# Values and softmax sums of two heads in one product, in the three attentions of a decoder kernel

## The chip, the cores and the metric

The kernel runs on one core of a Trainium2 chip. A core has a matmul engine (TensorE, PE in the profile, its weight loads PEld), VectorE (DVE), ScalarE (ACT), GpSimd (POOL), and SyncE (SP), which here only issues DMAs. The metric is the device time of one execution in microseconds (us); lower is better.

## What is computed

A decoder of two layers on 16 sequences of 256 tokens with 256 features, in float32: a differential causal self attention (32 heads of 16 features), a cross attention (16 heads), a mixture of experts, a state space block, a causal attention against the context (16 heads), and a feed-forward with low-rank experts, each with a residual and a layer norm. The change touches the three attentions. For each head they compute

```python
scores = q @ k.T / 4                   # 256 x 256, masked above the diagonal in self and causal
p = exp(scores - row_max(scores))
o = (p @ v) / p.sum(-1, keepdims=True) # 16 features a head
y = o_all_heads @ w_out
```

## The kernel before

Each attention is a software pipeline over the 16 batches. One pass of the loop body goes through `PAIRS` pairs of heads (16 in self, 8 in cross and causal, one "pair" `i` being one step of the body), and works on several batches at once: `st.has(d)` asks whether batch `st + d` exists, so `d = 3` is a batch whose projections are made, `d = 1` one whose row maxima are taken, `d = 0` one whose scores and products run, `d = -1` and `-2` batches on their way out. The order of work on each engine is written out by hand, as `if i == ...` in five `body` functions, one for each engine. Engines meet through counting semaphores.

For each pair:

- TensorE computes the scores of the pair into the single PSUM tile `score_ps` (`scores`, L522 in cross and causal, L1180 in self); it waits for `prob_ready` of the pair before.
- ScalarE takes the exponential into one of four `probs` buffers (`exponential`, L632, L1278). In self and causal GpSimd then zeroes the masked half of the diagonal blocks (`mask_probs`, L1494, L815).
- TensorE computes the score products of the next batch into one of two `max_ps` banks (`max_scores`), and VectorE takes the row maxima from them (`take_max`, L1415/L1416, L722). Four pairs' maxima are transposed (`transpose_max`), copied by ScalarE (`keep_max`) and sent into the row `TERMS` of the stacks by a small DMA from ScalarE's queue (`load_row`, L622, L1259), 4 KB and 8 KB. The first scores of each four pairs (i = 0, 4, ...) wait for that row.
- At every second pair TensorE runs `weighted` for a group `g` of two pairs: four heads in four 32-wide column tiles (`quad`). The parity `par` of the group says which half of the 32 rows of a quad holds the head. A tile of `out_ps` (128 rows, 512 columns) holds eight heads' values in its columns 0 to 255 and their softmax sums, from products with `ones`, in 256 to 511. Two groups (par 0 and 1) accumulate into it.

When both groups of a tile are there, ScalarE copies `out_ps` to `comb` (`keep_weighted`, L639, L1286), after the exponential of pair 2 or 6 (self also 10 and 14). VectorE inverts the sums and multiplies (`normalize`, L731 and L735, L1423 and L1427). GpSimd splits the result in a high and a low part (`part_o`, a cast and a subtraction, L824 and L826, L1503 and L1505), and TensorE projects it (`output` at i = 2 in cross and causal, `output_1` at i = 14 in self, by `product3`, L79 to L81). There are two tiles a batch in cross and causal and four in self. VectorE's `norm_rows` adds the residual and takes the moments, GpSimd takes `rstd` (`pow`), VectorE `shift_rows`, and ScalarE's `finish_rows` writes `y_out` (L648 at i = 6, L1310 at i = 7).

GpSimd in self also sorts a quarter of the queries twice a batch (`sort_q`, L1534, i = 1 and 9) and the keys (`sort_k`, L1525, i = 15), splits the queries (`split_q`, L1541, i = 6 and 8) and the low part of the keys (L1564, i = 11), and pads the values (`pad_v`, i = 10). ScalarE sorts the other quarters (L1269, i = 5 and 14) and rounds (L1301).

SyncE's order in cross and causal, for each pass: the residual rows, the next tokens and context, the first half of the stacks (which waits for `q_saved`), the store of `y_out` (which waits for `out_ready`), the save of k, the second half of the stacks, the save of q. Its queue is in order: what stands behind a wait waits too.

## Time and profile before

| | |
|---|---|
| time, median of 3 runs | 2770.53 us (2765.45 to 2774.43) |
| span of the profiled execution | 2765.9 us |
| TensorE busy | 2451.4 us (89%), weight loads 2025.2 us (73%) |
| VectorE busy | 1928.7 us (70%) |
| ScalarE busy | 1439.0 us (52%) |
| GpSimd busy | 1560.7 us (56%) |
| DMA | 363.48 MB, mean 131 GB/s |

The profile is of one execution; its time is its span, and no other time is given for it. Self attention fills its first 722 us, cross attention runs to about 1108 us, causal attention from about 2140 to 2510 us. Busy shares are means over stages whose limits differ, and an engine's idle time costs something only where the next engine waits for it. The granted clock (PEclk) is a share of TensorE's full 2.4 GHz; its two levels are 1.00 and 0.50.

### The profile page before, as it was taken

The page shows a single profiled execution, that of the slowest core. Times are in us where ns is not written, and L with a number is a line of the kernel's source. Part 1 is how long each engine was busy: PE and PEld are TensorE (multiplying, and loading weights), DVE is VectorE, ACT ScalarE, POOL GpSimd, SP SyncE. Part 2 cuts the span into 40 slices and gives each one's busy share as a digit, 9 for nine tenths or more (in the row PEclk, how much of TensorE's full clock was granted, in tenths as well). Part 3 has the DMA queues.
Part 4 walks back from the last instruction along what each step waited for, and adds up shares of the span by engine and source line. Part 5 has one row for each costly group of instructions (what it writes and reads, how often), then busy time and mean ns, then how long its engine had stood idle before and what let it go on. Part 6 is the DMA issues. An engine that isn't in the chain of part 4 may idle for free. (4 is left out here: it accounts for less than half of the span.)

```text
span 2765.9 us, 66315 instructions
## 1 busy us (share of the span) xinstructions
PE 2451.4 (89%) x24760; PEld 2025.2 (73%) x24760; DVE 1928.7 (70%) x3095; ACT 1439.0 (52%) x2255; POOL 1560.7 (56%) x1873
## 2 busy tenths in 40 slices
PE   5999999999589998898999994888896799997998
PEld 4676666676466665898999993677775577765998
DVE  2567666677367786364888885999985377775776
ACT  2565565565356665433665663656563355553333
POOL 3666565666345543056666664777765477764443
PEclk9999999999799999899999997999997899998999
DMA  8565555562477873024666663111000877761111
GB/s 200 124 152 138 130 146 117 144 146 68 122 193 203 208 193 93 31 89 160 217 230 221 216 217 118 37 39 47 24 13 29 238 192 207 209 146 35 58 57 50
DMA packets 228039, 363.48 MB, mean 131 GB/s; under 512 B 52848, under 2 KB 157168, under 8 KB 220272
## 3 DMA queue, kind: packets, MB, share of 16 engines
q1 hardware_dynamic: 207248, 281.28, 38.9%
q0 software_dynamic: 17376, 78.13, 8.0%
q8 instruction: 153, 2.51, 0.4%
q10 hardware_dynamic: 3200, 1.05, 0.2%
q14 instruction: 62, 0.51, 0.1%
HBM read 231.68 MB, written 133.69 MB: 132 GB/s over the span
## 5 line engine op out<-in xcount | busy, mean ns | idle before, releaser
L1278 ACT ACTIVATE self_probs<-self_score_ps 128x768 f32<-128x768 f32 x256 | 207.7, 811 | 218.7 <-PE self_score_ps L1180 215.7
L1494 POOL TENSOR_SCALAR_AFFINE_SELECT self_probs<-self_probs 128x512 f32<-128x512 f32 x256 | 167.7, 656 | 217.6 <-ACT self_probs L1278 217.4
L1415 DVE TENSOR_REDUCE self_neg_max<-self_max_ps 128x2 f32<-128x256 f32 x256 | 108.2, 422 | 227.1 <-PE self_max_ps L1166 223.6
L722 DVE TENSOR_REDUCE cross_neg_max<-cross_max_ps 128x4 f32<-128x1024 f32 x128 | 155.9, 1222 | 70.6 <-PE cross_max_ps L500 69.6
L632 ACT ACTIVATE cross_probs<-cross_score_ps 128x1024 f32<-128x1024 f32 x128 | 131.1, 1024 | 92.9 <-PE cross_score_ps L522 92.8
L1416 DVE TENSOR_REDUCE self_neg_max<-self_max_ps 128x2 f32<-128x512 f32 x256 | 174.5, 682 | 0.0
L2206 POOL TENSOR_TENSOR moee_h_lo<-moee_h,moee_h_hi 128x512 fp32r<-128x512 f32 x78 | 112.0, 1436 | 93.0 <-ACT moee_h_hi L1943 92.3
L3501 POOL TENSOR_TENSOR ffn_g_lo<-ffn_g_full,ffn_g_hi 128x512 fp32r<-128x512 f32 x64 | 82.2, 1284 | 129.4 <-ACT ffn_g_hi L3387 117.0
L1943 ACT ACTIVATE moee_h_hi<-moee_h 128x512 fp32r<-128x512 f32 x110 | 69.5, 632 | 164.2 <-DVE moee_h L2109 158.7
L632 ACT ACTIVATE causal_probs<-causal_score_ps 128x768 f32<-128x768 f32 x128 | 103.9, 811 | 95.0 <-PE causal_score_ps L522 94.9
L1180 PE MATMUL self_score_ps<-self_q_stack,self_k_stack 49*128 49x128 f32 (+1 forms) x1024 | 131.3, 336 | 24.7 <-issue 10.3
L79 PE MATMUL moee_g_ps<-moee_x_hi,moee_in_hi 128*128 128x256 f32 x440 | 132.2, 300 | 11.1 <-DVE moee_x_lo L2096 6.9
L1180 PEld LDWEIGHTS self_score_ps<-self_q_stack,self_k_stack 49*128 49x128 f32 x1024 | 79.0, 191 | 73.6 <-issue 40.0
L2109 DVE TENSOR_TENSOR moee_h<-moee_u_ps,moee_silu 128x512 f32<-128x512 f32 x110 | 75.6, 687 | 81.2 <-PE moee_u_ps L81 77.0
L1160 PE MATMUL self_max_ps<-self_k_stack,self_q_stack 48*128 48x128 f32 (+1 forms) x1024 | 108.2, 291 | 23.0 <-POOL self_k_stack L1525 22.0
L815 POOL TENSOR_SCALAR_AFFINE_SELECT causal_probs<-causal_probs 128x512 f32<-128x512 f32 x128 | 85.0, 664 | 75.7 <-ACT causal_probs L632 71.8
L79 PE MATMUL moee_y_ps<-moee_out_hi,moee_h_hi 128*128 128x256 f32 x440 | 125.3, 285 | 1.5 <-DVE moee_out_lo L2061 1.5
L81 PE MATMUL moee_g_ps<-moee_x_hi,moee_in_lo 128*128 128x256 f32 x440 | 126.4, 287 | 0.0
L80 PE MATMUL moee_g_ps<-moee_x_lo,moee_in_hi 128*128 128x256 f32 x440 | 126.3, 287 | 0.0
L2149 POOL DMA_INDIRECT x_tiles<-kept_x,moek_slot x64 | 65.8, 1029 | 106.7 <-issue 103.0
L79 PE MATMUL moee_u_ps<-moee_x_hi,moee_in_hi 128*128 128x256 f32 x440 | 125.5, 285 | 0.0
L81 PE MATMUL moee_u_ps<-moee_x_hi,moee_in_lo 128*128 128x256 f32 x440 | 125.0, 284 | 0.0
(500 smaller groups left out, 9667.4 us busy)
## 6 DMA issues: line engine op xcount, KB each, us to landing
self_q<-self_q_split SPq DMA_DIRECT2D x48, 512.0 KB, 3.2
self_q_raw<-self_q SPq DMA_DIRECT2D x32, 768.0 KB, 7.9
cross_stacks<-cross_qk SPq DMA_DIRECT2D x64, 384.0 KB, 6.6
causal_stacks<-causal_qk SPq DMA_DIRECT2D x64, 384.0 KB, 6.6
moe_y_tiles<-lasting_y_out SPq DMA_DIRECT2D x55, 256.0 KB, 2.5
mid<-lasting_y_out SPq DMA_DIRECT2D x48, 256.0 KB, 2.2
x_tiles<-zeros SPq DMA_DIRECT2D x16, 624.0 KB, 4.5
moee_xT<-x_tiles SPq DMA_DIRECT2D x39, 256.0 KB, 7.1
```

The source lines that it names most:

```text
L79: pe.matmul(out, a[0], b[0], start=start, stop=False, **kw)
L80: pe.matmul(out, a[0], b[1], start=False, stop=False, **kw)
L81: return pe.matmul(out, a[1], b[0], start=False, stop=stop, **kw)
L632: nc.scalar.activation(probs[i // 2][:, a, :, lo:], score_ps[:, :, lo:], ACT.Exp, scale=HD ** -0.5).then_inc(prob_ready, 1)
L722: last = dve.tensor_reduce(neg_max[p][:, tile, :, col % 4, :], bank[:].rearrange("p a (q k) -> p a q k", q=QT), AX.X, ALU.max, negate=True)
L1160: last = pe.matmul(max_ps[i % 2][:, ab, q * S:q * S + (q + 1) * P], q_stack[rows, 4 * tile + c, q * P:(q + 1) * P], k_stack[p][rows, tile, ...
L1180: last = pe.matmul(score_ps[:, ab, j * S + k * P:(j + 1) * S], k_stack[p][rows, tile, k * P:(k + 1) * P], q_stack[rows, 4 * tile + c, k * P:],
L1278: nc.scalar.activation(probs[g % 4][:, a, :, P:], score_ps[:, :, P:], ACT.Exp, scale=HD ** -0.5).then_inc(prob_ready, 1)
L1415: dve.tensor_reduce(neg_max[:, tile, :, c, 0:1], bank[:, :, 0:P], AX.X, ALU.max, negate=True)
L1416: dve.tensor_reduce(neg_max[:, tile, :, c, 1:2], bank[:, :, S:2 * S], AX.X, ALU.max, negate=True).then_inc(max_kept, 1)
L1494: pool.affine_select(diagonal, diagonal, [[0, 2], [0, 2], [1, P]], ALU.is_ge, zero, base=0, channel_multiplier=-1).then_inc(prob_masked, 1)
L2206: pool.tensor_tensor(h_lo[p][f][:].rearrange("p j s -> p (j s)"), h[f][:], h_hi[p][f][:].bitcast(F32).rearrange("p j s -> p (j s)"), ALU.s ...
```

## The change

A `weighted` group now has one set of eight matmuls instead of two. The unused half of each 32-column tile of `v_pad`, zero before, holds ones in every second of its 16 columns (the even ones for an even tile, the odd ones for an odd tile), so that the product gives the head's 16 values and, in eight of the other 16 rows, its softmax sum. The two groups of a tile no longer accumulate: par 0 goes to columns 0 to 255 of `out_ps`, par 1 to 256 to 511, and values and sums of the two lie in opposite halves of each 32 rows.

To bring them together, ScalarE (`cross_weighted`) copies `out_ps` with its two column halves exchanged and one row half zeroed by a column `scale`, into `crossed`. VectorE (`merge`) multiplies `out_ps` by the other column and adds `crossed`, into `merged`: values in one column half, sums in the other. A tile's sums sit in every second row, with zeros between them. GpSimd adds the sums of two tiles (`add_sums`, into `merged[0]`), VectorE inverts both at once (`invert`), and `normalize` spreads a tile's inverses over the rows, exchanging the row halves, with `stream_shuffle`, behind a one-column memset, and multiplies. `comb_ready`, which frees `out_ps` for TensorE, becomes `merged_ready`.

Places: `cross_weighted` stands ahead of the exponential of its pair, not behind it. `merge` is at the same pairs (2 and 6; 2, 6, 10, 14 in self); cross and causal: `add_sums` at 2, `invert` at 4, `normalize` at 5 and 6, `part_o` at 6 and 7 (before: normalize at 4 and 7, part_o at 3 and 5). Self: `add_sums` at 2 and 10, `invert` at 4 and 11, `normalize` at 5, 6, and both at 11 (before 3, 7, 11, 15), `part_o` at 6, 7, 12, 13 (before 0, 4, 8, 12). `pad_v` in self copies instead of adding zeros. The diff, cut to its core (cross and causal first, then self):

```diff
-        self.ones = m.sb("ones", [P, 2, 32])
+        self.halves = m.sb("halves", [P, 2])
...
-        comb = [m.sb(f"comb{i}", [P, 2, S]) for i in range(2)]
-        inv_sum = m.sb("inv_sum", [P, 2, S])
+        crossed = [m.sb(f"crossed{i}", [P, 2, S]) for i in range(2)]
+        merged = [m.sb(f"merged{i}", [P, 2, S]) for i in range(2)]
+        sums, inv_sum = merged[0][:, 1, :], merged[1][:, 1, :]
...
-                    pe.wait_ge(comb_ready, st.at(d) * 2 + tile)
-                for part in range(4):
-                    k = part % 2
-
+                    pe.wait_ge(merged_ready, st.at(d) * 2 + tile)
+                for k in range(QT):
                     first_q = P if causal and k == 1 else 0
                     cols = slice((1 - k) * S + first_q, (2 - k) * S)
                     for quad in range(4):
                         rows = slice(32 * quad, 32 * quad + 32)
-                        if part < 2:
-                            lhs = v_pad[p][:, k, tile * 4 + quad, par, :, :].rearrange("p a e -> p (a e)")
-                            out0 = 0
-                        else:
-                            lhs, out0 = ones[:, par, :], S
-                        last = pe.matmul(out_ps[rows, out0 + first_q:out0 + S], lhs,
+                        lhs = v_pad[p][:, k, tile * 4 + quad, par, :, :].rearrange("p a e -> p (a e)")
+                        last = pe.matmul(out_ps[rows, par * S + first_q:(par + 1) * S], lhs,
                                          probs[g][:, quad % 2, quad // 2, cols],
-                                         start=(par == 0 and part == 0),
-                                         stop=(par == 1 and part == 3), skip_group_check=True)
+                                         start=k == 0, stop=k == QT - 1, skip_group_check=True)
                 last.then_inc(pv_done, 1)
...
-            def keep_weighted(st, d, tile):
+            def cross_weighted(st, d, tile):
                 act.wait_ge(pv_done, st.at(d) * 4 + 2 * tile + 2)
                 if st.has(d - 1):
                     act.wait_ge(o_ready, st.at(d) * 2 + tile - 1)
-                nc.scalar.activation(comb[tile][:].rearrange("p a s -> p (a s)"), out_ps[:],
-                                     ACT.Identity).then_inc(comb_ready, 1)
+                nc.scalar.activation(crossed[tile][:, ::-1, :], out_ps[:].rearrange("p (a s) -> p a s", s=S),
+                                     ACT.Identity, scale=halves[:, 1:2]).then_inc(crossed_ready, 1)
...
+                    if i == 2 and st.has(-1):
+                        cross_weighted(st, -1, 1)
+                    if i == 6 and st.has(0):
+                        cross_weighted(st, 0, 0)
                     if st.has(0):
                         exponential(st, i)
...
-                    if i == 2 and st.has(-1):
-                        keep_weighted(st, -1, 1)
-                    if i == 6 and st.has(0):
-                        keep_weighted(st, 0, 0)
                     if i == 6 and st.has(-2):
                         finish_rows(st)
...
+            for t in range(2):
+                for tile in range(2):
+                    for par in range(2):
+                        ones = v_pad[t][:, :, 4 * tile:4 * tile + 4, par, 1 - par, tile::2]
+                        last = dve.memset(ones, 1.0)
+                last.then_inc(v_zeroed, 1)
...
+            def merge(st, d, tile):
+
+                dve.wait_ge(crossed_ready, st.at(d) * 2 + tile + 1)
+                if st.has(d - 1):
+                    dve.wait_ge(sums_ready, st.at(d))
+                    dve.wait_ge(o_ready, st.at(d) * 2 + tile - 1)
+                dve.scalar_tensor_tensor(merged[tile][:], out_ps[:].rearrange("p (a s) -> p a s", s=S),
+                                         halves[:, 0:1], crossed[tile][:], ALU.mult, ALU.add).then_inc(merged_ready, 1)
+
+            def invert(st, d):
+                dve.wait_ge(sums_ready, st.done(d))
+                dve.reciprocal(inv_sum, sums).then_inc(inv_ready, 1)
+
             def normalize(st, d, tile):
 
                 n = st.at(d) * 2 + tile
-                dve.wait_ge(comb_ready, n + 1)
-                dve.reciprocal(inv_sum[:, tile, :], comb[tile][:, 1, :]).then_inc(inv_ready, 1)
-                dve.wait_ge(inv_ready, n + 1)
+                dve.wait_ge(inv_ready, st.done(d))
+                dve.memset(gate[:], 0.0)
+                dve.stream_shuffle(crossed[tile][:, 1, :], inv_sum, [HD + tile] * HD + [tile] * HD).then_inc(scale_ready, 1)
+                dve.wait_ge(scale_ready, n + 1)
                 if st.has(d - 1):
                     dve.wait_ge(olo_ready, n - 1)
-                dve.tensor_tensor(o_full[:, tile, :], comb[tile][:, 0, :], inv_sum[:, tile, :],
+                dve.tensor_tensor(o_full[:, tile, :], merged[tile][:, 0, :], crossed[tile][:, 1, :],
                                   ALU.mult).then_inc(o_ready, 1)
...
+                    if i == 2 and st.has(-1):
+                        merge(st, -1, 1)
+                    if i == 6 and st.has(0):
+                        merge(st, 0, 0)
                     if i == 3 and st.has(-2):
                         norm_rows(st)
+                    if i == 4 and st.has(-1):
+                        invert(st, -1)
+                    if i in (5, 6) and st.has(-1):
+                        normalize(st, -1, i - 5)
                     if i == 5 and st.has(3):
                         dve.wait_ge(xhi_ready, st.done(3))
                         dve.tensor_tensor(x_lo[:].rearrange("p k s -> p (k s)"), misc[:],
@@ -772,10 +795,6 @@
                                           ALU.subtract).then_inc(xlo_ready, 1)
                     if i == 5 and st.has(-2):
                         shift_rows(st)
-                    if i == 4 and st.has(-1):
-                        normalize(st, -1, 1)
-                    if i == 7 and st.has(0):
-                        normalize(st, 0, 0)
...
+            def add_sums(st, d):
+                pool.wait_ge(merged_ready, st.done(d) * 2)
+                if st.has(d - 1):
+                    pool.wait_ge(inv_ready, st.done(d - 1))
+                pool.tensor_tensor(sums, merged[0][:, 1, :], merged[1][:, 1, :], ALU.add).then_inc(sums_ready, 1)
...
+                    if i == 2 and st.has(-1):
+                        add_sums(st, -1)
...
-                    if i == 3 and st.has(-1):
-                        part_o(st, -1, 0)
-                    if i == 5 and st.has(-1):
-                        part_o(st, -1, 1)
+                    if i in (6, 7) and st.has(-1):
+                        part_o(st, -1, i - 6)
...
+                    if i in (2, 6, 10) and st.has(0):
+                        cross_weighted(st, 0, i // 4 + 1)
+                    if i == 14 and st.has(1):
+                        cross_weighted(st, 1, 0)
...
-                    if i in (2, 6, 10) and st.has(0):
-                        keep_weighted(st, 0, i // 4 + 1)
-                    if i == 14 and st.has(1):
-                        keep_weighted(st, 1, 0)
...
-                    if i in (3, 7, 11) and st.has(0):
-                        normalize(st, 0, i // 4 + 1)
+                    if i in (2, 6, 10) and st.has(0):
+                        merge(st, 0, i // 4 + 1)
+                    if i in (4, 11) and st.has(0):
+                        invert(st, 0, i // 8)
+                    if i in (5, 6) and st.has(0):
+                        normalize(st, 0, i - 5)
+                    if i == 11 and st.has(0):
+                        normalize(st, 0, 2)
+                        normalize(st, 0, 3)
+                    if i == 14 and st.has(1):
+                        merge(st, 1, 0)
...
-                    if i == 15 and st.has(1):
-                        normalize(st, 1, 0)
...
+            def add_sums(st, d, half):
+                n = st.at(d) * 2 + half
+                pool.wait_ge(merged_ready, 2 * n + 2)
+                if half or st.has(d - 1):
+                    pool.wait_ge(inv_ready, n)
+                pool.tensor_tensor(sums, merged[0][:, 1, :], merged[1][:, 1, :], ALU.add).then_inc(sums_ready, 1)
...
-                    zeros = v_pad[p][:, :, par, 1 - par, :]
-                    pool.tensor_tensor(v_pad[p][:, :, par, par, :], v_nat[:], zeros,
-                                       ALU.add).then_inc(v_padded, 1)
+                    pool.tensor_copy(v_pad[p][:, :, par, par, :], v_nat[:]).then_inc(v_padded, 1)
...
-                    if i in (0, 4, 8, 12) and st.has(0):
-                        part_o(st, 0, i // 4)
+                    if i in (2, 10) and st.has(0):
+                        add_sums(st, 0, i // 8)
+                    if i in (6, 7, 12, 13) and st.has(0):
+                        part_o(st, 0, (6, 7, 12, 13).index(i))
...
-    a["ones"] = np.broadcast_to(np.repeat(np.eye(2), HD, axis=1), (P, 2, 2 * HD)).astype(np.float32)
+    a["halves"] = np.stack([i % 32 < HD, i % 32 >= HD], 1).astype(np.float32)
```

## Rows read from the trace of the kernel before

**Rows 1.** Busy time by stage; columns: PE, PEld, DVE, ACT, POOL, clock, DMA.
```profile
77.00:722.00 645.00, 601.65 (x7793) 436.78 (x7792) 432.61 (x767) 371.25 (x558) 389.18 (x509) 0.96 0.52 124
...
779.00:1108.00 329.00, 304.45 (x3764) 215.85 (x3762) 248.27 (x319) 201.82 (x296) 148.62 (x217) 0.99 0.69 174
```

**Rows 2.** TensorE in order of time in self: start, length, line, instructions.
```profile
387.25 0.83 PE L1205 MATMUL self_out_ps<-self_probs,lasting_ones 128*32 128x256 f32 x16
388.01 0.50 PE L1180 MATMUL self_score_ps<-self_q_stack,self_k_stack 49*128 49x128 f32 x4
...
395.37 0.50 PE L1180 MATMUL self_score_ps<-self_q_stack,self_k_stack 49*128 49x128 f32 x4
...
411.42 0.37 PE L79 MATMUL self_misc<-self_wo_hi,self_o_hi 128*128 128x256 f32 x1
```

**Rows 3.** ScalarE in order of time in self, pairs 5 and 6.
```profile
391.91 2.06 ACT L1269 ACTIVATE self_q_stack<-self_q_raw 128x1024 fp32r<-128x1024 f32 x1
...
394.38 0.81 ACT L1278 ACTIVATE self_probs<-self_score_ps 128x768 f32<-128x768 f32 x1
```

**Rows 4.** TensorE in self at the first max product of a batch; bracket: idle, releaser.
```profile
418.72 0.50 PE L1160 MATMUL self_max_ps<-self_k_stack,self_q_stack 48*128 48x128 f32 x4 [1.33 <-POOL self_k_stack L1525]
```

**Rows 5.** Busy time in two stretches of cross; last columns: clock, DMA share, GB/s.
```profile
938.00:950.00 12.00, 11.13 (x135) 8.29 (x136) 8.83 (x14) 6.02 (x10) 5.73 (x10) 1.00 1.04 265
953.00:956.00 3.00, 3.00 (x36) 2.60 (x36) 1.94 (x3) 2.49 (x5) 2.64 (x4) 1.00 0.00 0
```

**Rows 6.** SyncE's longest wait in cross: total us, times, longest.
```profile
SPq L396 <- ACT lasting_y_out L648: 132.5, 15, 15.9
```

**Rows 7.** TensorE in order of time in cross.
```profile
940.66 1.05 PE L547 MATMUL cross_out_ps<-cross_probs,lasting_ones 128*32 128x256 f32 x16
941.63 0.51 PE L522 MATMUL cross_score_ps<-cross_stacks 49*128 49x256 f32 x4
...
947.39 0.50 PE L522 MATMUL cross_score_ps<-cross_stacks 49*128 49x256 f32 x4 [0.87 <-DMA cross_stacks<-cross_max_row]
```

**Rows 8.** Instructions of ScalarE's copy in self; ns min/median/max, first and last start.
```profile
L1286 ACT ACTIVATE self_comb<-self_out_ps x64: 575/592/620, 86.2 to 711.1; 128x512 f32<-128x512 f32 x64
```

**Rows 9.** ScalarE's groups in self: busy us, mean ns, idle before.
```profile
L1310 ACT ACTIVATE lasting_y_out<-self_r,self_shift,self_rstd 128x256 f32<-128x256 f32 x30 | 16.5, 610 | 0.0
```

**Rows 10.** VectorE in order of time in self, pairs 3 to 5.
```profile
387.62 0.68 DVE L1437 TENSOR_TENSOR self_r<-self_misc,self_x_res 128x512 f32<-128x512 f32 x1
...
389.52 1.75 DVE L1423 RECIPROCAL self_inv_sum<-self_comb 128x256 f32<-128x256 f32 x1
391.31 0.42 DVE L1427 TENSOR_TENSOR self_o_full<-self_comb,self_inv_sum 128x256 f32<-128x256 f32 x1
391.65 0.42 DVE L1415 TENSOR_REDUCE self_neg_max<-self_max_ps 128x2 f32<-128x256 f32 x1
...
392.58 0.42 DVE L1415 TENSOR_REDUCE self_neg_max<-self_max_ps 128x2 f32<-128x256 f32 x1
```

**Rows 11.** GpSimd's groups in self: busy us, mean ns, idle before.
```profile
L1494 POOL TENSOR_SCALAR_AFFINE_SELECT self_probs<-self_probs 128x512 f32<-128x512 f32 x253 | 165.8, 656 | 210.4 <-ACT self_probs L1278 210.2
L1534 POOL CAST self_q_stack<-self_q_raw 128x1024 fp32r<-128x1024 f32 x30 | 60.1, 2002 | 0.0
L1505 POOL TENSOR_TENSOR self_o_lo<-self_o_full,self_o_hi 128x256 fp32r<-128x256 f32 x64 | 46.8, 731 | 5.4
L1541 POOL TENSOR_TENSOR self_q_split<-self_q_full,self_q_split 128x512 fp32r<-128x512 f32 x26 | 33.3, 1279 | 0.0
...
L1503 POOL CAST self_o_hi<-self_o_full 128x256 fp32r<-128x256 f32 x64 | 25.2, 394 | 34.4 <-DVE self_o_full L1427 34.4
...
L1564 POOL TENSOR_TENSOR self_k_split<-self_k_full,self_k_split 128x256 fp32r<-128x256 f32 x14 | 10.2, 728 | 0.0
```

**Rows 12.** Busy time and clock in self behind the wait of rows 4.
```profile
420.00:424.00 4.00, 4.00 (x39) 2.38 (x42) 2.22 (x5) 1.41 (x2) 2.94 (x4) 0.50 0.43 96
```

**Rows 13.** TensorE at the end of cross, its last output product.
```profile
1103.47 0.55 PE L79 MATMUL cross_misc<-cross_w_hi,cross_o_hi 128*128 128x256 f32 x1 [5.66 <-POOL cross_o_lo L826]
```

More of the change, by code:

```diff
@@ L1191, in weighted @@
                 if par == 0 and (tile or st.has(d - 1)):
-                    pe.wait_ge(comb_ready, st.at(d) * TILES + tile)
-                for part in range(4):
-                    k = part % 2
+                    pe.wait_ge(merged_ready, st.at(d) * TILES + tile)
+                for k in range(QT):
                     first_q = P if k == 1 else 0
```

66 lines of the change are left out of this document (42 added, 24 removed).

## The prediction

> **What bounds the kernel now.** I read the stages first, then each engine in order of time inside one batch, then waits. In the stage table [rows 1] TensorE is busy for 602 of 645 us in self attention and 304 of 329 us in cross attention; causal attention reads like cross. One would say: TensorE bound, take its work away and time falls with it. The views in order of time say otherwise. TensorE's order is written by hand and each pair's scores go through one PSUM tile, so scores i+1 wait for ScalarE's exponential i. What fills TensorE between two scores is cover for the other engines, and three things behind that cover are nearly as long as it is:
>
> - ScalarE in self, pairs 5 and 6: the q_stack copy (2.06 us) and a rounding stand ahead of exponential 6, which ends at 394.38 + 0.81 = 395.19; TensorE's next scores start at 395.37 [rows 2, 3]. Slack 0.2 us.
> - GpSimd in self: TensorE stands 1.33 us before the max products of the next batch, until sort_k is done [rows 4]. That chain (exponential 15, mask, sort_k) hangs on scores 15, not on the product behind them.
> - The DMA engines in cross (and causal): 1.04 share, 265 GB/s, for 12 us, then 0.00 for 3 us [rows 5]. The burst starts when the y_out store, which SyncE waits for (132.5 us in 15 waits), is released by finish_rows at pair 6 [rows 6]. The small row of maxima that scores 4 need lands when the burst has drained: TensorE waits 0.87 us for it [rows 7].
>
> **The products.** Per group of pairs eight matmuls with `ones` (16 records in the trace) go. In self they take 388.01 - 387.25 = 0.76 us, in cross 941.63 - 940.66 = 0.97 us [rows 2, 7]. Groups: 8 x 16 = 128 in self, 4 x 16 = 64 in cross and 64 in causal (priced as self: it too skips the masked half). Ceiling: 128 x 0.76 + 64 x 0.97 + 64 x 0.76 = 97 + 62 + 49 = 208 us. Part of each 0.76 is the turn to the next scores, which stays; I walk with 0.7 and 0.9.
>
> **The added work.** ScalarE's copy becomes one of the same size with a scale column and swapped halves: 0.59 us [rows 8]; no row has a scaled 128x512 copy, so between 0.59 and twice the 0.61 us of finish_rows' scaled 128x256 (1.22) [rows 9]; I take 0.6, since only a column is added. It also moves ahead of the exponential of its pair. merge on VectorE (128x512, PSUM and SBUF) is nearest to self_r, 0.68 us [rows 10]. add_sums on GpSimd is like o_lo, 0.73 us [rows 11]. The reciprocal (1.75 us) runs half as often: 4 to 2 per batch in self, 2 to 1 in cross and causal. The shuffle (128x256) has no row: 0.42 us as the multiply of the same size, which reads one tensor more, up to the reciprocal's 1.75 [rows 10]; below 0.42 I see nothing, as every 256-column row of VectorE is at least that. I take 0.42, since a shuffle does no arithmetic. VectorE per self batch: -2 x 1.75 + 4 x 0.68 + 4 x 0.42 = +0.9 us; cross and causal: -1.75 + 2 x 0.68 + 2 x 0.42 = +0.45. In self, pad_v's two adds (as k_low, 0.73) become copies (as o_hi's cast, 0.39 [rows 11]): 0.7 us off GpSimd. The eight setup memsets lie beside the weights' loading, and the new memset of one column rides in front of each shuffle.
>
> On the shuffle, the Trainium skill ("VectorE: DVE Perf Modes", The perf-mode tier table) says that it exists only in the one-element-per-cycle mode. Its formula for fp32 tensor_tensor gives an estimated 0.42 us at 256 columns; the multiply's row agrees, and no run here shows a shuffle yet.
>
> **Self, walked from scores 4 (time 0).** Now scores 7 start at 395.37 - 388.01 = 7.36 [rows 2]. With product 3 shorter, norm_rows ends on VectorE 0.6 later relative to scores 4 than now (reciprocal start, 389.52 - 388.01 = 1.51 [rows 10]), at 2.1. Then take_max 4 (392.58 - 391.65 = 0.93 [rows 10]) to 3.0, invert to 4.8, take_max 5 to 5.7, shift_rows to 6.1, shuffle and multiply of tile 0 to 7.1. The new copy of pair 6 waits for exactly that (o_ready), and exponential 6 stands behind it: 7.1 + 0.6 + 0.8 gives scores 7 at 8.6. So the product at pair 5 saves nothing, and 1.3 us are lost.
> From there GpSimd decides. Until output_1 (pair 14) it has 8 masks x 0.66, 4 part_o x (0.39 + 0.73) instead of 2, 2 split_q x 1.28, sort_q 2.0, k_low 0.73, pad_v 0.8 and add_sums 0.73 [rows 11]: 5.3 + 4.5 + 2.6 + 2.0 + 0.7 + 0.8 + 0.7 = 16.6 us. TensorE needs now 411.42 - 395.37 = 16.05 [rows 2], after four shorter products 16.05 - 2.8 = 13.3. So TensorE stands about 3 us in front of output_1, partly already before max_scores 14, because invert and two normalizes hold VectorE at pair 11 for 1.75 + 2 x 0.9 = 3.6 us in front of take_max 12. That makes output_1 1.3 + 0.7 = 2.0 us later than now. Product 15 is hidden by sort_k. Products 1 and 3 of the next batch save 1.4 together, more where the clock is low. Net per batch: 0, from -0.5 to +1. Five of eight shortened products are eaten where they stand, the others pay back what the chain lost.
>
> **Cross and causal.** Products 1 and 3 lie between scores 0 and scores 4, which wait for the drained burst: both save nothing and the wait grows from 0.87 to about 2.5 us. The burst starts with finish_rows, behind exponential 6, behind the new copy, behind o_ready of tile 0: from scores 4, take_max 4 ends at 2.0, invert 3.8, take_max 5 4.9, normalize 5.9, copy 6.5, exponential 7.5. Against now this is 0.2 us (cross) to 0.4 us (causal, whose take_max is shorter) earlier, though products 5 and 7 save 1.8. The loop burst, scores 4, finish_rows closes with a gain of 0.2 to 0.4 per batch.
>
> **The clock.** After a 1.33 us idle stretch the granted clock is 0.50, 1.2 instead of 2.4 GHz, for the next 4 us [rows 4, 12]. A mean clock of 0.96 over self's 645 us [rows 1] is 52 us at half rate, 3 us in each of 16 batches, while the 0.87 us of rows 7 leaves 1.00. The change makes idle stretches of 2 to 3 us in front of output_1 and in front of scores 4 of cross and causal, where TensorE is then on the path. Four us at half rate cost up to 2 us each. Charged at half, with less where chains of other engines cover it: self +1.0, cross +0.5, causal +0.4 per batch net of the gains above.
> The Trainium skill ("TensorE: Matmul & The Clock Gate", HAM oscillation) says that waits between groups of matmuls let the gate fall, so that each next group starts at half rate. That is the rule that speaks against removing matmuls without removing the wait; the 0.50 row agrees.
>
> **Stage ends.** After the last product the chain to the output grows by merge 0.7, add_sums 0.7, shuffle and multiply of a second tile 0.9 and a second part_o 1.1, less what ran beside: TensorE's 5.66 us wait [rows 13] becomes about 8. Three stages: +6.
>
> **Sum.** With 14 full batches in self and 13 each in cross and causal: 14 x 1.0 + 13 x 0.5 + 13 x 0.4 + 6 = 14 + 6.5 + 5 + 6 = +31 us. The profiled execution's span is 2765.9 us, 4.6 under the median of the three runs (2770.5), as near as the runs stand to each other. 2765.9 + 31 = 2797, against the median 2802; I say 2800. A measurement of this kernel can tell about 0.3%, 8 us, from no change.
>
> **Rivals.** (a) The chains hold as walked but no further stretch loses its clock: self 0, cross -13 x 0.2, causal -13 x 0.4, ends +6: 2768 (2755 to 2778). Against it: the 1.33 us stretch already costs the clock. (b) Faster: tile 0 is normalized before TensorE reaches pair 6, so the copy never waits and finish_rows moves with TensorE. It decides if VectorE finishes 1.1 us earlier. Then products 5 and 7 pay in cross and causal (26 x 1.5 = 40 us) and in self about 2 of the 8 products (14 x 1.5 = 21), less some clock: 2705, from 2660 to 2745. For it: VectorE idles elsewhere in each batch. Against: the order in its queue is fixed. The floor is the DMA work, about 17 of 21 us in cross. (c) Worse: scaled copy 1.2 us or shuffle 1.75 us: each tile adds 0.6 or 1.3 to the chain before exponential 6 or output_1; 40 batches x 1 to 1.5 us on top of the forecast: 2850. (d) TensorE is the bound after all: 128 x 0.7 + 64 x 0.9 + 64 x 0.7 = 192 us less, 2580.
>
> **Chances.** Forecast 0.43 (2780 to 2830, slower); (a) 0.24 (same 0.15, faster 0.06, slower 0.03); (b) 0.23; (c) 0.06; (d) 0.04. Sum: faster 0.33, same 0.15, slower 0.52. The range 2715 to 2835 leaves out (c), (d) and a part of (b), about 2 in 10.
>
> **What the profile after would show.** 4,096 matmul records fewer and TensorE busy some 190 us less; VectorE about 16 x 0.9 + 32 x 0.45 = 29 us more; exponential 6 in self and finish_rows behind o_ready of tile 0; in cross a wait of 2 us or more at scores 4 for the row of maxima with a clock of 0.50 behind it; in self a wait at max_scores 14 or output_1. I am wrong if the y_out store in cross comes over 1 us earlier in its batch, if output_1 starts without a wait, or if idle stretches of 2 us keep the clock at 1.00.

## The result and the profile after

The changed kernel needs 2857.9 us (median of 4 runs, 2850.6 to 2863.6), the kernel before, on the same chip, 2770.6. The ratio is 1.031 (95% interval 1.028 to 1.033): 87 us slower, where 31 were forecast and the range ended at 2835. The profiled execution took 2852.6 us with a span of 2850.7 and a mean granted clock of 0.891 (before 0.943).

The page of the changed kernel, busy times and the line of the granted clock:

```profile
PE 2405.1 (84%) x20664; PEld 1985.6 (70%) x20664; DVE 1956.0 (69%) x3567; ACT 1453.6 (51%) x2255; POOL 1590.2 (56%) x1937
...
PEclk8788888888779998799999997999998799987999
```

The 4,096 matmul records are gone, yet TensorE is busy for only 46 us less, not 190: what is left runs slower. The windows by stage give the place (columns as in [rows 1]). First self attention from its first to its last exponential, then the same for cross, then causal:

```profile
65.00:762.00 697.00, 601.41 (x5749) 432.38 (x5751) 439.81 (x986) 380.54 (x562) 400.10 (x539) 0.83 0.47 115
828.00:1153.00 325.00, 273.39 (x2721) 199.93 (x2719) 251.36 (x412) 206.56 (x298) 157.94 (x230) 0.90 0.68 178
...
2256.00:2580.00 324.00, 283.93 (x2967) 208.59 (x2969) 233.87 (x531) 187.25 (x324) 235.28 (x355) 0.93 0.68 180
```

Between the same two instructions the kernel before took 640.7, 320.8 and 314.2 us, the changed one 696.7, 325.2 and 323.8: self +56, cross +4, causal +10. The stretch between cross and causal took 12 us more. Three of these are the end of cross itself, where TensorE waits longer for its last output product (before 5.66 us, [rows 13]); the other 9.5 lie in stages that the change does not touch. The other seams and the end make up the rest of the 85 us between the two spans. The end of cross in the changed kernel:

```profile
1166.54 0.56 PE L79 MATMUL cross_misc<-cross_w_hi,cross_o_hi 128*128 128x256 f32 x1 [7.37 <-POOL cross_o_lo L851]
```

TensorE in order of time in one self batch of the changed kernel, the counterpart of [rows 2] and [rows 4]:

```profile
409.00 0.50 PE L1207 MATMUL self_score_ps<-self_q_stack,self_k_stack 49*128 49x128 f32 x4
...
417.24 0.49 PE L1207 MATMUL self_score_ps<-self_q_stack,self_k_stack 49*128 49x128 f32 x4 [1.40 <-ACT self_probs L1298]
...
432.71 0.80 PE L1187 MATMUL self_max_ps<-self_k_stack,self_q_stack 48*128 48x128 f32 x4 [2.09 <-DVE self_neg_max L1443]
...
434.19 0.55 PE L79 MATMUL self_misc<-self_wo_hi,self_o_hi 128*128 128x256 f32 x1
...
438.96 0.51 PE L1207 MATMUL self_score_ps<-self_q_stack,self_k_stack 49*128 49x128 f32 x4
...
443.19 0.50 PE L1187 MATMUL self_max_ps<-self_k_stack,self_q_stack 48*128 48x128 f32 x4 [1.96 <-POOL self_k_stack L1580]
```

Scores 4 stand at 409.00 (the next at 453.38), scores 7 at 417.24, output_1 from 434.19 to 438.96. The brackets are the three idle stretches: before scores 7, before max_scores 14, before max_scores 0. The same batch in windows, with the granted clock ahead of the last two columns:

```profile
408.00:430.00 22.00, 20.13 (x243) 14.35 (x242) 17.35 (x41) 16.13 (x26) 15.10 (x22) 1.00 0.57 161
430.00:432.00 2.00, 0.62 (x12) 0.30 (x4) 1.93 (x8) 1.12 (x2) 1.45 (x3) 0.83 0.47 132
432.00:434.00 2.00, 1.29 (x6) 0.64 (x6) 1.58 (x4) 2.00 (x2) 1.92 (x4) 0.50 0.88 263
434.00:436.00 2.00, 1.85 (x9) 1.84 (x9) 1.68 (x3) 0.14 (x1) 0.64 (x2) 0.50 0.87 207
436.00:438.00 2.00, 2.00 (x12) 2.00 (x11) 0.00 (x0) 0.00 (x0) 0.00 (x0) 0.50 0.54 55
438.00:440.00 2.00, 2.00 (x22) 1.53 (x25) 0.00 (x0) 0.93 (x2) 0.00 (x0) 0.97 0.00 0
...
444.00:448.00 4.00, 4.00 (x40) 2.36 (x37) 2.64 (x5) 2.20 (x4) 1.94 (x2) 0.62 0.48 104
```

The clock is 1.00 until the idle stretch before max_scores 14, then 0.50 (1.2 GHz) through the first three quarters of output_1, and it falls again behind the wait for k_stack. TensorE's waits in self (total us, times, longest) show that this is every batch, not one:

```profile
PE self_score_ps L1207 <- ACT self_probs L1298: 33.7, 36, 3.9
PE self_max_ps L1187 <- POOL self_k_stack L1580: 28.1, 15, 2.0
PE self_max_ps L1187 <- DVE self_neg_max L1443: 27.9, 14, 2.1
```

ScalarE ahead of scores 7, and VectorE ahead of max_scores 14:

```profile
415.80 0.69 ACT L1306 ACTIVATE self_crossed<-self_out_ps,lasting_halves 128x512 f32<-128x512 f32 x1 [0.28 <-DVE self_o_full L1469]
416.38 0.80 ACT L1298 ACTIVATE self_probs<-self_score_ps 128x768 f32<-128x768 f32 x1
```
```profile
428.04 1.75 DVE L1458 RECIPROCAL self_merged<-self_merged 128x256 f32<-128x256 f32 x1 [1.04 <-POOL self_merged L1551]
...
431.25 0.47 DVE L1469 TENSOR_TENSOR self_o_full<-self_merged,self_crossed 128x256 f32<-128x256 f32 x1
431.64 0.41 DVE L1442 TENSOR_REDUCE self_neg_max<-self_max_ps 128x2 f32<-128x256 f32 x1
```

The scaled copy waits for o_ready and holds exponential 6; invert and two normalizes hold VectorE from 428.0 to 431.6 in front of take_max 12. In cross, scores 4 now wait 1.75 us per batch for the row of maxima (before: [rows 7]); total, times, longest:

```profile
PE cross_score_ps L524 <- DMA cross_stacks<-cross_max_row: 22.7, 13, 2.3
```

### The profile page after: what moved, and what is told of

The parts are those of the page before. It is cut to its first block and busy times, and to the rows that moved or that the text cites. A ratio compares the mean times of both kernels' runs of the same rounds, so it can differ in the third digit from the quotient of the medians.

```text
span 2850.7 us, 58943 instructions
## 1 busy us (share of the span) xinstructions
PE 2405.1 (84%) x20664; PEld 1985.6 (70%) x20664; DVE 1956.0 (69%) x3567; ACT 1453.6 (51%) x2255; POOL 1590.2 (56%) x1937
## 5 line engine op out<-in xcount | busy, mean ns | idle before, releaser
L1187 PE MATMUL self_max_ps<-self_k_stack,self_q_stack 48*128 48x128 f32 (+1 forms) x1024 | 120.0, 317 | 63.6 <-POOL self_k_stack L1580 35.5
L1207 PE MATMUL self_score_ps<-self_q_stack,self_k_stack 49*128 49x128 f32 (+1 forms) x1024 | 140.0, 355 | 38.7 <-ACT self_probs L1298 33.7
L1207 PEld LDWEIGHTS self_score_ps<-self_q_stack,self_k_stack 49*128 49x128 f32 x1024 | 85.5, 207 | 93.5 <-ACT self_probs L1298 47.4
L1187 PEld LDWEIGHTS self_max_ps<-self_k_stack,self_q_stack 48*128 48x128 f32 x1024 | 92.0, 216 | 72.2 <-DVE self_neg_max L1443 31.1
L1226 PE MATMUL self_out_ps<-self_probs,self_v_pad 128*32 128x256 f32 (+1 forms) x2048 | 126.1, 370 | 3.6 <-POOL self_probs L1543 1.8
```

What stands on the lines that cost most here:

```text
L1187: last = pe.matmul(max_ps[i % 2][:, ab, q * S:q * S + (q + 1) * P], q_stack[rows, 4 * tile + c, q * P:(q + 1) * P], k_stack[p][rows, tile, ...
L1207: last = pe.matmul(score_ps[:, ab, j * S + k * P:(j + 1) * S], k_stack[p][rows, tile, k * P:(k + 1) * P], q_stack[rows, 4 * tile + c, k * P:],
L1226: last = pe.matmul(out_ps[rows, par * S + first_q:(par + 1) * S], lhs, probs[g % 4][:, quad % 2, quad // 2, cols], start=k == 0, stop=k == ...
```

## The experiments

Theory 1: the loops are held by handovers; the products saved were work in their shadow, and the new idle stretches of about 2 us halve the clock for the work behind them, which is the loss. Theory 2: the longer handovers are the loss and the clock only goes along. Theory 3: TensorE's own work still counts. Fifteen kernels were run, each against the kernel before on the same chip, and the ratio is to that. The kernel before had medians from 2766.8 to 2776.1 us there, so differences between the times of two rows are rougher than those of the ratios. The columns by stage are of one profiled execution each; that of twice lies 21 us over its median, that of copy_behind 9 over, that of filled 5 under. "Self, steady" is from the first exponential to the last x_hi copy (there is one per batch, for its projections; this is the 16th), "self, end" from there to the last exponential: the batches in which no projections are left. All from each run's profile, in us; the clock is self's.

| kernel | time | ratio (interval) | self, steady | self, end | clock | cross | causal |
|---|---|---|---|---|---|---|---|
| before | 2766.8 to 2776.1 | 1 | 519.3 | 121.4 | 0.95 | 320.8 | 314.2 |
| after | 2857.9 | 1.031 (1.028 to 1.033) | 556.6 | 140.1 | 0.83 | 325.2 | 323.8 |
| fill_gaps | 2812.7 | 1.017 (1.015 to 1.019) | 534.6 | 139.6 | 0.91 | 319.6 | 317.3 |
| twice | 2807.2 | 1.013 (1.011 to 1.016) | 539.1 | 134.0 | 0.94 | 329.5 | 325.2 |
| before_no_sums | 2778.1 | 1.004 (1.002 to 1.005) | 497.1 | 135.5 | 0.88 | 324.9 | 325.9 |
| copy_behind | 2811.6 | 1.014 (1.010 to 1.017) | 542.2 | 135.8 | 0.83 | 324.8 | 317.7 |
| late_norms | 2876.5 | 1.037 (1.034 to 1.040) | 569.0 | 147.8 | 0.83 | 327.6 | 329.5 |
| self_only | 2833.0 | 1.020 (1.018 to 1.022) | 555.6 | 143.7 | 0.82 | 318.6 | 311.8 |
| cross_only | 2791.5 | 1.006 (1.003 to 1.009) | 637.0 in all | | 0.96 | 326.8 | 328.0 |
| mended | 2815.8 | 1.014 (1.011 to 1.016) | 536.1 | 139.6 | 0.89 | 316.2 | 312.6 |
| output_late | 2805.9 | 1.015 (1.012 to 1.018) | 517.2 | 136.5 | 0.86 | 325.3 | 327.3 |
| all_mended | 2762.9 | 0.998 (0.997 to 1.000) | 500.6 | 132.6 | 0.87 | 316.0 | 314.1 |
| before_late | 2776.2 | 1.002 (1.001 to 1.004) | 650.6 in all | | 0.97 | 322.8 | 314.6 |
| before_fill | 2766.0 | 0.999 (0.997 to 1.001) | 632.1 in all | | 0.98 | 322.8 | 313.3 |
| filled | 2754.8 | 0.996 (0.995 to 0.998) | 488.9 | 131.0 | 0.92 | 316.5 | 313.9 |
| filled_twice | 2767.1 | 1.000 (0.999 to 1.001) | 630.1 in all | | 0.92 | 322.0 | 312.5 |
| no_sums_filled | 2742.6 | 0.992 (0.991 to 0.994) | 495.0 | 122.4 | 0.93 | 312.6 | 310.9 |

**fill_gaps.** Is the idle clock the loss, or only its sign?

```diff
-                        weighted(st, 1, i // 2 - 5)
+                        weighted(st, 1, i // 2 - 5, 1 if i == 11 else 3)
-                        weighted(st, 0, i // 2 - 1)
+                        weighted(st, 0, i // 2 - 1, 3 if i == 3 else 1)
```


> The changed kernel with the products of pairs 13 and 15 of the self attention, and of pair 3 of the other two, issued three times each (the repeats write the same numbers): about 3 us more of TensorE's work in a self batch, put where the changed kernel's TensorE stood idle for about 2 us before max_scores 14 and again before the last wait for k_stack. Theory 1 (the short idle stretches let the granted clock fall, and that is the loss): the clock of the self stage comes back from 0.83 to 0.90 or more, output_1 takes about 3.2 us instead of 4.8, and the kernel needs about 2800 us (2780 to 2825). Theory 2 (the longer chains of handovers are the loss, the clock only shows it): no gain, 2855 to 2870. Theory 3 (TensorE's own work is the bound): 3 us more in 15 batches, about 2900.

2812.7: more work, 45 us less time (39 by the ratios). Theory 2 in its pure form and theory 3 are out. But only 22 of self's 56 us came back with the clock at 0.91: the wait before scores 7 stayed, and output_1 took 3.04 us in seven batches but about 4.5 in eight, where theory 1 expected 3.2 in all.

**twice.** Every `weighted` of the three attentions runs its products two times (`times=2`).

> The changed kernel with every product issued twice (the repeat writes the same numbers), so that TensorE's work is about that of the kernel before, with the new handovers unchanged. Theory 1 (clock): the work itself costs nothing, the clock of the self stage comes back to above 0.92, and about two thirds of the 87 us are won back: about 2800 us (2780 to 2830). Theory 2 (handovers alone): as after or slightly more, 2855 to 2880. Theory 3 (TensorE's work is the bound): up to 6 us more in each self batch, 2900 to 2960.

2807.2, in theory 1's range: 4,096 more matmul records than after, and 51 us faster (48 by the ratios). It also shows what theory 1 leaves out. In self it has as many matmuls as the kernel before and almost its clock (0.94, before 0.95), and output_1 is back at 3.04 us, yet self takes 673 us, 32 more than before:

```profile
66.00:739.00 673.00, 616.68 (x7759) 442.46 (x7759) 441.21 (x985) 380.56 (x561) 400.45 (x538) 0.94 0.49 120
```

So the new handovers have a price apart from the clock, most of these 32 us: 20 lie in the steady part, 1.5 per batch, and 13 at the end (the execution is one above the median). In cross and causal the doubled products brought nothing (329.5 and 325.2, after 325.2 and 323.8).

**before_no_sums.** The saving without the handovers.

```diff
-                for part in range(4):
+                for part in range(2):
+            dve.memset(out_ps[:, S:2 * S], 1.0)
```


> The kernel before without the products with the ones; its sums are left out (that half of the accumulator holds ones), and nothing else is changed, so no new handover comes in. It is the saving alone. Theory 1 (the products taken away were work in the shadow of handovers, and without them the clock falls): 2740 to 2790, with the granted clock of the self stage below the 0.96 of before. Theory 2 (the saving is real, and the new handovers eat it): 2600 to 2680 with the clock near 0.96.

2778.1: slower than before by 0.4%, with 4,096 matmul records fewer and nothing added. Its windows, self without its end and the end, and below them the end in the kernel before:

```profile
67.00:564.40 497.40, 451.41 (x4639) 323.73 (x4638) 349.49 (x612) 302.69 (x459) 318.11 (x412) 0.91 0.60 141
564.40:700.00 135.60, 123.22 (x1108) 82.98 (x1108) 86.28 (x156) 70.31 (x103) 70.84 (x98) 0.76 0.32 75
```
```profile
586.40:707.80 121.40, 113.24 (x1540) 79.17 (x1540) 86.05 (x158) 69.89 (x102) 72.86 (x101) 0.99 0.36 84
```

In the steady batches the saving is worth 22 us. At the end, where no projections fill TensorE, it costs 14, with the clock at 0.76 instead of 0.99. Cross and causal lose the 4 and 12 us that the whole change loses there (4 and 10), which leaves next to nothing for the new handovers of these two.

**copy_behind.** `cross_weighted` is moved behind `exponential` in both bodies of ScalarE.

> The changed kernel with the scaled copy (cross_weighted) issued behind its pair's exponential instead of ahead of it, in all three attentions; this takes the wait for o_ready and the 0.69 us copy out of the path to exponential 6 of the self attention and delays the merge by up to 0.8 us. Theory 1 (clock) and theory 2 (handovers) both allow a gain where that handover sets the pace: about 1.4 us of the 1.40 us wait before scores 7, of which the rest of the batch gives back most: 2835 to 2860. If the order of copy and exponential were the main loss, 2800 or less.

2811.6, 46 us less, where up to 23 were expected (the ratio, 1.014, stands well under the 1.024 to 1.033 of the expectation). The profile shows 32 of them: self -19 (1.2 per batch) at nearly the same clock (0.83), causal -6, and -8 between cross and causal. So most of the gain in self comes from the handover itself.

**late_norms.**

```diff
-                    if i == 11 and st.has(0):
+                    if i == 12 and st.has(0):
                         normalize(st, 0, 2)
                         normalize(st, 0, 3)
```


> The changed kernel with the self attention's normalizes of tiles 2 and 3 issued behind take_max 12 instead of ahead of it. The wait before max_scores 14 is 2.1 us in the changed kernel; it should shrink to under 0.5, and GpSimd's part_o(3) and with it output_1 come up to 0.9 us later. Theory 1 (short idle stretches cost mostly through the clock): the fall of the clock at output_1 goes with the wait, output_1 takes about 3.2 us instead of 4.8, the self stage's clock rises to 0.88 or more, and the loop of 15 batches gains 20 to 40 us: 2820 to 2840. Theory 2 (only the length of the handovers counts): 0 to 15 us gained, 2843 to 2858. If output_1 waits for its own input instead, the idle stretch moves there and the clock stays at 0.83: 2850 to 2865.

2876.5: both theories missed. The third case of the expectation has the mechanism, but it is dearer than 2850 to 2865. The wait before max_scores 14 went, and a longer one came, for o_lo:

```profile
PE self_misc L79 <- POOL self_o_lo L1561: 42.9, 13, 3.3
```

The two normalizes sit on two chains, to take_max 12 and through part_o to output_1; one order serves one of them.

**self_only and cross_only.** The attention functions of before and after are exchanged whole.

> The changed self attention with the cross and causal attentions of before (they need the table of ones again). In the profiles the change lengthened the self products by 56 us, cross by 4, causal by 10 and the stages between by 12. Theory 1: the parts add up, 2826 if the 12 us belong to cross or causal, 2838 if they follow from the self stage. Rival (the slower self stage is partly made up by what follows): 2800 to 2815.

> The self attention of before with the changed cross and causal attentions. Theory 1: 4 us from cross and 10 from causal, 2782 to 2786; the kernel before without its sums (products with ones left out, no new handover) lost the same 4 and 12 us there at a clock of 0.90 and 0.91, so the new handovers of these two cost nothing. If the 12 us of the stages between belong to the changed cross attention, 2795.

2833.0 and 2791.5, +57 and +15 against the kernel before on the same chip (2776.1). Together 72 of the 87: self has four fifths of that. self_only lies between the two values of its theory 1, cross_only between its two cases. In the profile of cross_only the two stages show 6 + 14 us, and the stretch between them 10 more, which self_only (2 more) does not have.

**mended.** copy_behind and late_norms, with the product of pair 15 (self) and of pair 3 (cross, causal) issued three times.

> The changed kernel with three edits at once: the scaled copy behind its pair's exponential (all three), the normalizes of tiles 2 and 3 behind take_max 12 (self), and a product issued three times where TensorE waits (pair 15 of self, pair 3 of cross and causal; the repeats write the same numbers). By the runs so far the first gave 46 us back and repeats 45. If the two act on different losses: 2745 to 2785, with a self stage of 640 us or less and a clock above 0.90. If both act on the same loss: 2795 to 2810.

2815.8, a miss. Cross and causal came to 316.2 and 312.6, under the kernel before; self kept late_norms' wait for o_lo (42.8 us in 13).

**output_late.** late_norms, and output_1 with its y_hi one pair later:

```diff
-                    if i == 14 and st.has(0):
+                    if i == 15 and st.has(0):
                         output_1(st)
```


> The changed kernel with the self attention's output_1 (and the copy y_hi behind it) one pair later, behind product 15, and the normalizes of tiles 2 and 3 behind take_max 12. With the normalizes moved alone, output_1 waited 3.3 us for part_o(3); a pair later that input is there, and output_1's 3.2 us fill the 2.0 us in which max_scores 0 waits for sort_k. Theory (the chain to output_1 and the k_stack wait are the two idle stretches that lengthen the batch and let the clock fall): both waits go, the self clock rises to 0.90 or more, self comes from 697 down to 650 to 665, and the kernel needs 2805 to 2825. Rival (the GpSimd chain itself, sums to part_o to mask to sort_k, sets the period): self stays at 685 or more, 2845 to 2860.

2805.9. Self -43 us: the steady part is 517.2, as before, and the wait for k_stack is down to 1.1 us in one batch. Output_1 fills that wait, and its input has a pair more time. The clock stayed at 0.86, where 0.90 or more was expected.

**all_mended.** output_late, copy_behind, and the product of pair 3 of cross and causal three times.

> The edits of output_late, with the scaled copy behind its pair's exponential in all three attentions and the product of pair 3 issued three times in cross and causal. Cross and causal were 316 and 313 us with the latter two (321 and 314 in the kernel before). Theory: self's losses are separate (copy ahead of the exponential about 20 us, chain to output_1 and clock the rest), so self is 630 to 645 and the kernel needs 2750 to 2785. Rival: one loss is only moved to the other wait, self stays at 660 or more, 2790 or more.

2762.9, with an interval that ends just under 1 (0.9996). Self is 633.2, as in before_no_sums (632.6): -43 and -20 add up to the 64 us that lie between the saving alone and the changed kernel. One fall per batch is left, here in order of time and by windows:

```profile
322.73 0.50 PE L1187 MATMUL self_max_ps<-self_k_stack,self_q_stack 48*128 48x128 f32 x4 [1.03 <-DVE self_neg_max L1443]
...
324.41 1.41 PE L1226 MATMUL self_out_ps<-self_probs,self_v_pad 128*32 128x256 f32 x16 [0.85 <-DVE self_merged L1453]
```
```profile
322.00:324.00 2.00, 0.82 (x6) 0.41 (x6) 2.00 (x5) 2.00 (x2) 1.91 (x4) 1.00 1.01 309
324.00:328.00 4.00, 3.59 (x26) 2.98 (x27) 1.19 (x3) 0.30 (x1) 3.16 (x4) 0.57 0.50 87
```

**before_late and before_fill.** output_1 at pair 15, and the product of pair 15 issued twice, each alone in the kernel before.

> The kernel before with nothing of the change but output_1 and y_hi of the self attention one pair later. Its k_stack wait was 15.6 us in 12 batches. Theory: output_1 fills that wait, 5 to 15 us gained: 2755 to 2770. Rival: the wait is the end of a chain through GpSimd and stays: 2768 to 2780.

> The kernel before with the product of pair 15 of the self attention issued twice (the same numbers again), 1.55 us of work in front of the wait for k_stack of up to 1.4 us. Theory 1 (an idle stretch costs through the clock): clock of the self stage from 0.95 to 0.98 or more and 5 to 15 us gained, 2755 to 2768. Rival (work is work): 0.2 to 1.5 us more per batch, 2772 to 2795.

2776.2 and 2766.0. Late output_1 is worth nothing by itself, which the theory missed: the wait for k_stack goes and 20.8 us of waits for comb take its place. Self is 10 us longer at a clock of 0.97, higher than before. The repeat took self to 632.1 in the profiled execution, but the times cannot be told from no change.

**filled, filled_twice, no_sums_filled.** all_mended with the self product of pair 13 three times, or of pairs 13 and 15 twice; and before_no_sums with those of pair 15 (self) and pair 3 (cross, causal) three times.

> The kernel all_mended with the self attention's product of pair 13 issued three times (the same numbers again): 1.5 us of work in front of max_scores 14, where TensorE waited 1.0 us, and 0.85 us more at product 15, after which the clock fell to 0.50 for about 3 us in every batch. Theory 1 (the fall is what is left): self's clock from 0.87 to 0.95 or more, self 610 to 625 us, 2740 to 2755, faster than both kernels. Rival (VectorE's chain at pairs 11 to 15 sets that place): product 15 waits as before, self 630 to 640, 2760 to 2772.

> The kernel all_mended with the self attention's products of pairs 13 and 15 issued twice each, the same 1.5 us of work, but half of it behind the wait for merged. Theory 1: the idle stretch at pair 14 is halved only, the fall stays in some batches: 620 to 635 in self, 2750 to 2768. Rival: as for filled.

> The kernel before without the products with the ones (sums left out, that half of the accumulator holds ones), and with the product of pair 15 of self and of pair 3 of cross and causal issued three times, in front of the waits for sort_k and for the row of maxima. Theory 1 (the saving alone is eaten by the clock): self's clock from 0.88 to 0.95 or more, self from 633 to 605 to 620, cross and causal from 325 and 326 to 312 to 318: 2725 to 2750. Rival (handovers bound the batch whatever the clock is): 2765 to 2780.

filled needs 2754.8, 0.36% under the kernel before and 103 us under the changed one (95 by the ratios): of the complete versions it is the one that is clearest under both. Against all_mended its self stage is 13 us shorter in the profiles, but the ratios (0.998 and 0.996) give the repeats only about 5, with intervals that overlap. Its steady part in self:

```profile
64.00:553.10 489.10, 449.00 (x5055) 325.35 (x5055) 345.04 (x779) 302.87 (x460) 326.62 (x434) 0.95 0.59 145
```

filled_twice, with half of the same work behind the wait for merged instead of in front of max_scores 14, is at 1.000. Its self clock is 0.92 as in filled, and still self takes 10 us more: the mean clock alone does not tell the time. no_sums_filled is 2742.6: with the clock held by repeats, a part of the saving shows, 24 us against the kernel before (of the 208 that the products were priced at) and 35 against before_no_sums, from self's end (135.5 to 122.4), cross (324.9 to 312.6) and causal (325.9 to 310.9). Self's steady part hardly moved (497.1 to 495.0) though its clock rose from 0.91 to 0.94.

## Why the prediction was wrong in size

**What held.** The direction, and its reason: the kernel's time is not TensorE's work, so taking work away does not shorten it: before_no_sums shows that outright (self's steady part gains 22 us, the other stretches lose more), and rival (d) was 280 us off. Rival (b) fell with the copy's wait for o_full, 27.2 us in 28 times in self; rival (a) with the clock. A product became 0.64 us shorter (scores follow after 0.79 us instead of 1.43), 0.7 was walked with. The unit costs: scaled copy 0.687 us (0.6 taken), merge 0.742 (0.68), shuffle 0.440 (0.42), add_sums 0.732 (0.73); VectorE's busy time rose by 27 us (29). These leave rival (c) no ground: the copy is 0.09 dearer, not 0.6, and that its 2850 lies nearest to the measured time is chance. The walk: scores 7 came 8.24 after scores 4 (8.6), output_1 25.19 (1.8 later than before; 2.0 walked), 2.1 us of idle before max_scores 14 (3). From the end of output_1 to the next scores 4 the batch gained 1.4 us, as walked. The cost of the copy's place, 1.3 us per batch in the walk, is what copy_behind gave back (1.2). In cross scores 4 wait 1.75 us (2.5), and the stages lost 4 + 10 = 14 us (6.5 + 5). The end of each attention, from its last exponential to its last matmul, grew by 2.7 to 2.9 us, 8 in all (+6). The idle stretch of self stood before max_scores 14, one of the two places that were named; output_1 itself then hardly waited (1.0 us in 3 times), which the prediction had called a sign of being wrong. One slip of its arithmetic: (a) counts its changes from the median before, 2770.5, the forecast and (b) from the span, 2765.9; from the span (a) is 2764, well inside its range.

**The step that failed** is the clock's price in self: "Charged at half, with less where chains of other engines cover it: self +1.0", worked out from one further stretch of four us at half rate in each batch. Windows of one period each (from one x_hi copy to the next), three of the kernel before and then three of the changed one, give its size:

```profile
131.20:170.30 39.10, 37.60 (x505) 27.98 (x504) 27.93 (x51) 24.35 (x37) 25.62 (x34) 1.00 0.60 146
...
420.00:464.20 44.20, 40.56 (x505) 29.75 (x504) 27.74 (x52) 24.40 (x37) 24.67 (x33) 0.92 0.55 130
464.20:504.90 40.70, 39.05 (x503) 28.62 (x502) 27.90 (x52) 24.43 (x37) 26.32 (x35) 0.96 0.60 141
```
```profile
136.90:178.40 41.50, 35.69 (x376) 26.22 (x376) 28.44 (x65) 24.65 (x38) 26.11 (x35) 0.92 0.57 138
178.40:222.90 44.50, 38.56 (x382) 28.41 (x378) 28.41 (x65) 24.81 (x38) 26.14 (x35) 0.85 0.51 128
...
400.50:444.80 44.30, 38.24 (x376) 28.00 (x376) 28.52 (x65) 24.79 (x38) 26.14 (x35) 0.85 0.52 128
```

Output_1 of the walked batch of before ran from 411.42 [rows 2] to the scores behind it:

```profile
414.47 0.50 PE L1180 MATMUL self_score_ps<-self_q_stack,self_k_stack 49*128 49x128 f32 x4
```

A mean clock of 0.96 over 40.7 us is (1 - 0.96) / 0.5 x 40.7 = 3.3 us at half rate; 0.85 over 44.3 us is 13.3. So 10 us more per batch at half rate, not 4: the stretch from output_1 on, and another behind the wait for k_stack, where pairs 0 to 2 run at 1.2 GHz (product 1 takes 1.51 us, as long as a product took with its sums at full rate). The batch of before that was walked (scores 4 at 388.01 to the next at 430.29) had such a second stretch too, most others had less. Against that batch the shown one of after (409.00 to 453.38) is 2.1 longer: the walk without the clock gives 1.8 - 1.4 = +0.4, output_1 at half rate 4.77 - 3.05 = +1.7, and nothing covers output_1. Against the mean of all 13 periods, 41.3 before and 44.2 after, it is +2.8 per batch where +1.0 was charged: 37 us. The 0.7 between the two is mostly that the walked batch of before was itself 1.0 longer than its mean.

**A term that was missing** is self's end: +19 us in the last batches (121.4 to 140.1, clock 0.99 to 0.81). The sum counted 14 full batches and gave the rest no price. Without projections between the pairs nothing covers the chain to exponential 6; that wait is 3.9 us there, 1.4 in a full batch. before_no_sums loses 14 of the 19 with no new handover, so most of it is again the removed work and the clock. With 37 + 19 = 56 self is accounted for, against 14 forecast, and that is the miss: the other terms, 4 + 10 + 8, came to 22 (forecast 17.5), and the last 6 of the 85 us lie mostly in the stages between.

**Handover or clock.** The two are not separate sums: a handover that is late by 2 us costs those 2 us, and then what the low clock makes of the work behind it. The kernel twice has the new handovers with the number of products and nearly the clock of before: of self's 56 us it keeps 32, and 24 go with the emptier TensorE and its lower clock. In the steady part it keeps 20 of 37, 1.5 per batch. By the walk the shorter products give about 1 of that back (+0.4 is left), and the clock then costs more than they gave. Reordering alone, with the same work, took 64 us off self; repeats alone 22; in all_mended repeats took another 13 in the profiles. The Trainium skill ("TensorE: Matmul & The Clock Gate", HAM oscillation) names waits between groups of matmuls as what makes the gate fall; by that rule the changed kernel should swing in each batch, and the trace agrees: in the batch shown the clock falls behind two of three waits, and ten periods in a row have a mean of 0.85. The example there in the Trainium skill has DMA waits of 3 to 5 us; here waits of about 2 us were enough, and in the kernel before one of 1.33 [rows 4, 12].

**Still open.** The 9.5 us in the unchanged stages between cross and causal. In the fifteen experiments the whole stretch, with the end of cross in it, took from 1088 to 1100 us (before 1090, after 1102), in no order that follows the edits. self_only and cross_only fall 15 us short of 87 together; the cause of that remainder was not found.

## What to carry to other kernels

Before taking matmuls out, ask what else they cover: in a loop whose period is set by handovers, shorter work on TensorE turns into idle stretches, and these can be paid twice, in waiting and in a halved clock for the work behind them. Run the saving alone first (leave the work out, add nothing): if that gives no time, as here, the change must come with a reordering that shortens the waits. And price the batches without filler at the loop's end apart from the steady ones.

## What the runs showed of the hardware

Identical matmuls written again, in front of a wait, can make a kernel faster: 39 to 45 us in fill_gaps, while in filled (ratio 0.998 to 0.996) the gain is small beside the intervals. Where they stand counts: with half of the same 1.5 us behind the wait (filled_twice) the ratio is 1.000, against 0.996 on the same chip.

The length of one idle stretch does not tell whether the clock falls. Behind a 1.96 us wait for k_stack it fell to 0.62 in the changed kernel (444 to 448), yet before_no_sums kept 1.00 behind the same wait:

```profile
326.70 0.50 PE L1161 MATMUL self_max_ps<-self_k_stack,self_q_stack 48*128 48x128 f32 x4 [1.96 <-POOL self_k_stack L1527]
```
```profile
324.00:332.00 8.00, 6.04 (x73) 4.25 (x66) 6.97 (x11) 3.67 (x6) 6.68 (x7) 1.00 0.39 68
```

In the kernel before, a wait of 1.33 us had 0.50 behind it [rows 4, 12]. The changed kernel had been idle for 2.09 us and at half rate 10 us earlier, before_no_sums had not; whether that is what makes the difference is not shown.
